# Adaptive-norm attention with mixture and zone feed-forward on one core: group 0's q and k laid at 32 rows a head, maxima from 24-row matmuls, the other layouts filled by DMA

## The chip, the core and the metric

The kernel runs on one core of one Trainium2 chip. The metric is the device time of one execution in microseconds (us). The kernel before takes 181.37 us, the median of 3 runs (181.26 to 181.59).

## The reference, cut to what matters

```python
def _L0_attn_ref(x, w_qkv, w_out):          # x: (2, 512, 128), 16 heads of 8
    q, k, v = jnp.split(x @ w_qkv.T, 3, axis=-1)
    q, k = _apply_rope(q, cos, sin), _apply_rope(k, cos, sin)
    scores = jnp.einsum('bhsd,bhtd->bhst', q, k) / scale
    scores = jnp.where(causal, scores, -jnp.inf)
    attn = jax.nn.softmax(scores, axis=-1)
    ...
    return out @ w_out.T

x = x + _L0_attn_ref(_L0_cond_ref(x, cond, weight), w_qkv, w_out)
x = x + _L0_ffn_ref(_L0_cond2_ref(x, cond, ...), ...)   # experts, then the zones chosen by a router
```

The change lies in the first microseconds of the attention, in the scores of batch 0's first four heads.

## The kernel before, in words

**Groups.** 2 batches times 16 heads are worked on in 8 groups of 4 heads (`HG = 4`, `GROUPS = 8`). Each q and k is split into a high part and a low part, both in the reduced-precision float32 format fp32r, and three part products make a score. So a head takes 8 x 3 = 24 rows (`PARTS * HD`), and a group 96 rows (`TOP`). Sequence length is 512, cut in blocks of 128.

**Two passes over the scores.** For each group TensorE first computes the scores with queries on the output partitions ("maxima units", `scores_for_max`, L1407, or L1402 for a unit of four heads), and VectorE masks and reduces each to the row maxima (`reduce_max`, L772). Then the maxima go through `max_pad` and a small matmul (`lay_max_under_q`, L1420) as 8 further rows under q. Last TensorE computes the scores again with keys on the output partitions and the maximum already subtracted (`scores_for_exp`, L1443, L1447, L1452), ScalarE takes the exponential (L1105), GpSimd masks the diagonal blocks (L672), and `weigh_v` (L1467) multiplies with v. The maxima units of group n + 1 lie between those of the exponential of group n, in an order written out by hand. Three PSUM banks in a ring hold the maxima units, so a unit waits until the unit three places before it is reduced. Of group 0's 12 maxima units all but u = 0 and u = 7 have one dummy matmul ahead (`keep_warm`, L1286).

**Layouts of q and k.** A group needs four of them. `stacked[0:96, n, :]` is k, the moving operand of the maxima units. `q_pad[n % 2]` is q once for each head, with the 72 rows of the other heads at zero, so that a 96-row matmul against all of k gives one head's scores. `q_mov[n % 3]` is q unmasked, and `k_pad[n % 3]` is k once for each head with zeros elsewhere; the exponential's matmuls use these two. For groups 1 to 7 all four are loaded by DMA from a copy in DRAM that `spill` writes from `qk_hi` and `qk_lo`. Group 0 does not go through DRAM (`BY_PE = 1`): `stack_half` (L1380, L1381) makes its 96 rows by matmul with a 0/1 pattern, in two halves of 256 columns, and ScalarE copies them out of PSUM: `place_q0(j, h)` (L1056) eight times into `q_pad[0]` with a per-row 0/1 scale, `copy_k0(h)` (L1061) into `stacked`, `copy_q0(h)` (L1065) into `q_mov[0]`. Only `k_pad[0]` is filled by DMA, from `stacked`: `pad_k(0, pairs)` (L446), two heads each time.

**SyncE's queue.** SyncE issues nearly all DMAs, strictly in the order of its program, and a wait holds up everything behind it. After group 1's spill and its loads comes: `load_k(1)`, `pad_k(0, (1,))`, `spill(sp, 2, NG, 0, spilled)` (q of groups 2 and 3 to DRAM, L390 and L393), `load_q(1)` (L461), `load_k(2)` (L455), the wait for q's spill, `pad_q(2)` (four DMAs, L433), `pad_k(1)`, `load_q(2)`, and so on. k's spill of groups 2 and 3 is issued from ScalarE's queue. `scores_for_max(2, 0)` is the first matmul that needs `pad_q(2)`. In TensorE's order it comes after group 1's twelfth maxima unit and before `scores_for_exp(0, 4)`.

Of the kernel before, what the change touches and what calls it, by code (L numbers as in the profile page):

```python
# [14 lines left out]
P = 128  # L15
# [121 lines left out]
def f32_of(ap):  # L137

    return ap.bitcast(F32)
# [7 lines left out]
def program(nc, io, scratch, out):  # L147
# [9 lines left out]
    with ctx:  # L157
# [55 lines left out]
        w_qk = raw[:, 2 * S:2 * S + 4 * D].rearrange("p (i t d) -> p i t d", i=2, t=2)  # L213
        w_v = raw[:, 2 * S + 4 * D:2 * S + 5 * D]
        w_cond = raw[:, 2 * S + 5 * D:2 * S + 6 * D]
        at = 2 * S + 6 * D
# [66 lines left out]
        def sum_of(i):  # L283
# [7 lines left out]
            pads_early ys_ready sq_ready dsum_ready dinv_ready mod_ready exp_set dvar_ready cond_ready  # L291
            qk_ready v_ready v_copied rope_ready roped_ready hi_ready lo_ready sel_zero sel_ready causal_zero q1_zero k2_zero pads_zero ones_out q_last_ready q0_placed pj_copied v_ones
            const_ready rep_ready rep_copied mx_full mx_reduced mhi_ready m_ready qm_full qm_copied st_full
# [8 lines left out]
         pads_early, ys_ready, sq_ready, dsum_ready, dinv_ready, mod_ready, exp_set, dvar_ready, cond_ready,  # L302
         qk_ready, v_ready, v_copied, rope_ready, roped_ready, hi_ready, lo_ready, sel_zero, sel_ready, causal_zero, q1_zero, k2_zero, pads_zero, ones_out, q_last_ready, q0_placed, pj_copied,
         v_ones, const_ready, rep_ready, rep_copied, mx_full, mx_reduced, mhi_ready, m_ready, qm_full, qm_copied,
# [10 lines left out]
        spilled = [sem(f"spilled_{x}") for x in "qk"]  # L315
        ld_stack = {n: [sem(f"ld_stack{x}{n}") for x in "qk"] for n in range(BY_PE, GROUPS)}
        stored = [sem(f"stored{s}") for s in range(2)]
# [65 lines left out]
        def spill(queue, first, last, i, done):  # L383
# [9 lines left out]
            queue.dma_start(parts[:, lo, :], f32_of(qk_lo[q, i, :])).then_inc(done[i], 16)  # L393

        def head_rows(j):

            return slice(j * PARTS * HD, (j + 1) * PARTS * HD)
# [15 lines left out]
        def _(sp):  # L413
# [21 lines left out]
            def pad_k(n, pairs=(0, 1)):  # L435

                s = n % BUFS
                if n >= BUFS:
                    sp.wait_ge(st_full, (n - 2) * STU)
                for h2 in pairs:  # L440
                    if n < BY_PE:
                        sp.wait_ge(rep_copied, 3)
                    for j in (2 * h2, 2 * h2 + 1):
                        q = head_rows(j)
                        src = f32_of(stacked[q, n, 0:3 * P]) if n < BY_PE else laid(n, 1)[q, 0:3 * P]
                        sp.dma_start(f32_of(k_pad[s][q, j, 0:3 * P]), src).then_inc(k_padded[s][h2], 16)  # L446

            def set_ones(s):

                sp.dma_start(f32_of(k_pad[s][TOP:ROWS, :, :]), ones_dram.rearrange("(r j) t -> r j t", j=HG)  # L450
                             ).then_inc(ones_rows[s], 16)

            def load_k(n):
# [65 lines left out]
            load_k(1)  # L519
            pad_k(0, (1,))  # L520
            spill(sp, 2, NG, 0, spilled)
            load_q(1)
            sp.wait_ge(spilled[1], 16 * SPILLS)
            load_k(2)
            sp.wait_ge(spilled[0], 16 * SPILLS)
            pad_q(2)
            sp.wait_ge(pads_zero, 2)
# [63 lines left out]
        def _(pool):  # L591
# [57 lines left out]
            def spread_last_queries(n):  # L649

                pool.wait_ge(qm_copied, n + 1)
                if n == 0:
                    pool.wait_ge(ld_head, 16)
                    pool.wait_ge(rep_copied, 4)
                else:
                    pool.wait_ge(st_full, STU * n)
                    pool.wait_ge(ld_stack[n][0], 16)
                G.tensor_tensor(q_last[0:ROWS], f32_of(q_mov[n % BUFS][0:ROWS, 3 * P:S]).unsqueeze(1).broadcast_to([ROWS, HG, P]),
                                head_mask[0:ROWS].unsqueeze(2).broadcast_to([ROWS, HG, P]),
                                ALU.mult).then_inc(q_last_ready, 1)  # L660
# [362 lines left out]
        def _(act):  # L1023
# [27 lines left out]

            def place_q0(j, h):
                act.wait_ge(rep_ready, 2 * h + 1)
                if (j, h) == (0, 0):
                    act.wait_ge(ld_const, 32)
                A.activation(q_pad[0][0:TOP, j, half(h)], first_stack(0, h)[0:TOP, :], ACT.Identity,  # L1056
                             scale=consts[0:TOP, C_HEAD + j:C_HEAD + j + 1]).then_inc(q0_placed, 1)

            def copy_k0(h):
                act.wait_ge(rep_ready, 2 * h + 2)  # L1060
                A.copy(stacked[0:TOP, 0, half(h)], first_stack(1, h)[0:TOP, :]).then_inc(rep_copied, 1)  # L1061

            def copy_q0(h):
                act.wait_ge(rep_ready, 2 * h + 1)
                A.copy(q_mov[0][0:TOP, half(h)], first_stack(0, h)[0:TOP, :]).then_inc(rep_copied, 1)  # L1065

# [139 lines left out]
            modulated(1, xc[:, 1, :], psum[:, 2, :])  # L1206
            place_q0(0, 0)
            copy_k0(0)
            take_hi_half(0, 1)
            place_q0(1, 0)  # L1210
            take_hi_half(1, 1)
            place_q0(2, 0)
            place_q0(3, 0)
            copy_q0(0)
            copy_k0(1)
            for j in range(HG):
                place_q0(j, 1)
            A.activation(minus_ident_b[:], consts[:, C_ID:C_MASK], ACT.Identity, scale=-1.0)
            A.copy(ident_r[:], consts[:, C_ID:C_MASK]).then_inc(const_ready, 1)
            copy_projection(0)  # L1220
            copy_q0(1)
            copy_v(0)
            spill(act, 2, NG, 1, spilled)
            copy_projection(1)
# [54 lines left out]
        def _(pe):  # L1279
# [25 lines left out]
            def wait_slot(*item):  # L1305

                k = ST_ORDER.index(item)
                if k < 2:
                    pe.wait_ge(q0_placed, 2 * HG)
                    pe.wait_ge(rep_copied, 4)  # L1310
                    return
                kind, n, *u = ST_ORDER[k - 2]
                if kind == "exp":
                    pe.wait_ge(exp_done, STU * n + u[0] + 1)
                else:
                    pe.wait_ge(pj_copied, n + 1)

            def wait_ring(*item):

                k = RING_ORDER.index(item)  # L1320
                if k < len(RING_BANKS):
                    if k == 1:
                        pe.wait_ge(xc_ready[1], 1)
                    elif k == 2:
                        pe.wait_ge(rep_copied, 1)
                    return
                kind, n, *u = RING_ORDER[k - len(RING_BANKS)]
                if kind == "max":
                    pe.wait_ge(mx_reduced, units_to(n, u[0] + 1))
                else:  # L1330
                    pe.wait_ge(qm_copied, n + 1)
# [23 lines left out]
            def project_v(b):  # L1355
                if b == 0:
                    pe.wait_ge(xc_ready[0], 1)
                    pe.wait_ge(q0_placed, HG)
                    pe.wait_ge(rep_copied, 2)
                else:  # L1360
                    pe.wait_ge(v_copied, KB)
# [21 lines left out]
            def scores_for_max(n, u):  # L1383
                s = n % 2
                pieces = MX_UNITS[n][u]
                if n == 0:
                    if u < 2 * HG:
                        pe.wait_ge(q0_placed, u + 1)
                    if u in (0, HG):
                        pe.wait_ge(rep_copied, 3 if u else 1)  # L1390
                elif u == 0:
                    pe.wait_ge(q_padded[s], 16 * HG * ((n + 1) // 2))
                    pe.wait_ge(ld_stack[n][1], 16)
# [4 lines left out]
                if len(pieces) == HG:  # L1398
                    pe.wait_ge(ld_stack[n][0], 16)
                    for padded in k_padded[n % BUFS]:  # L1400
                        pe.wait_ge(padded, 32 * (n // BUFS + 1))
                    last = T.matmul(bank.rearrange("p (j k) -> p j k", j=HG), q_mov[n % BUFS][0:TOP, 0:P],  # L1402
                                    k_pad[n % BUFS][0:TOP, :, 0:P], start=True, stop=True)
                else:
                    for j, qb, o in pieces:
# [18 lines left out]
            def scores_for_exp(n, u):  # L1424
                s = n % BUFS
                c, h2 = divmod(u, 2)
                if u == 0:
                    pe.wait_ge(qm_copied, n + 1)
                    if n == 0:
                        pe.wait_ge(rep_copied, 4)  # L1430
                    else:
                        pe.wait_ge(ld_stack[n][0], 16)
                    if n < BUFS:
                        pe.wait_ge(ones_rows[s], 16)
# [14 lines left out]
                else:  # L1449
                    pe.wait_ge(q1_zero, 2)  # L1450
                    pe.wait_ge(q_last_ready, n + 1)
                    last = T.matmul(ST[:, at_, :].rearrange("p (j q) -> p j q", j=HG), stacked[0:ROWS, n, 3 * P:S],  # L1452
# [246 lines left out]
def host_constants():  # L1699

    pattern = np.zeros((4, 32, P), np.float32)
    for j in range(HG):
        for d in range(HD):
            src = j * HD + d
            for t, parts in enumerate(((0, 1), (2,), (0, 2), (1,))):
                for r in parts:
                    pattern[t, src, (j * HD + d) * PARTS + r] = 1.0
    consts = np.zeros((P, C_END), np.float32)
# [71 lines left out]
```

## Time and profile before

| | |
|---|---|
| median of 3 runs | 181.37 us |
| profiled execution, its own time | 180.98 us |
| span of its trace | 179.1 us |
| TensorE busy | 168.9 us, 94% |
| VectorE busy | 138.9 us, 78% |
| ScalarE busy | 134.3 us, 75% |
| GpSimd busy | 93.8 us, 52% |
| chain that ended last, TensorE's share | 70% |

A profile line names the line of the kernel, the engine, the operation and the tiles it writes and reads. "SPq" is SyncE's queue: the time there is what it takes to issue a DMA, not to carry it out. Matmul ends are modelled, so neighbouring matmuls seem to overlap. "Landing" is the time from the issue of a DMA to its semaphore.

### The profile page before, as it was taken

Reading aid. Unit: us, or ns where it says so; the run is one execution under the profiler, and the core shown is the slowest. Engines: PE = TensorE matmul, PEld = TensorE weight load, DVE = VectorE, ACT = ScalarE, POOL = GpSimd, SP = SyncE. Lnnn points to the kernel's source line nnn. Section 1 sums busy time; section 2 is a strip of 40 time slices with the busy share of each in tenths; the row PEclk is TensorE's granted clock in tenths of the full one; section 3 lists DMA queues with packets and bytes.
Section 4 is the critical chain, followed back from the end, with each engine's and each line's share of the span. In section 5 each row is a group of like instructions: output and inputs, shape, how many; then the busy total and the mean of one; then the engine's idle time right before and its main releaser. Section 6 shows DMA issues by size and latency. Waiting matters only on the chain.

```text
span 179.1 us, 3278 instructions
## 1 busy us (share of the span) xinstructions
PE 168.9 (94%) x943; PEld 116.8 (65%) x944; DVE 138.9 (78%) x444; ACT 134.3 (75%) x224; POOL 93.8 (52%) x117
## 2 busy tenths in 40 slices
PE   6899999899999999988999999996999989999992
PEld 2656575565666666653758767864687867788881
DVE  5588989989898899980586999699799658637551
ACT  3569177688768888889734787953879999999970
POOL 5508088985463969688532522021769931676000
PEclk9999999999999999999999999999999999999999
DMA  4824775676686567520110899960760000001001
GB/s 144 294 46 107 191 203 159 218 234 213 166 267 208 143 194 194 164 94 5 62 51 17 231 345 344 347 178 4 241 230 0 0 4 0 0 2 59 0 4 59
DMA packets 15349, 24.28 MB, mean 136 GB/s; under 512 B 2844, under 2 KB 4828, under 8 KB 15308
## 3 DMA queue, kind: packets, MB, share of 16 engines
q1 hardware_dynamic: 14532, 23.29, 42.2%
q10 hardware_dynamic: 800, 0.79, 1.7%
q8 instruction: 8, 0.13, 0.3%
q14 instruction: 9, 0.07, 0.1%
HBM read 18.71 MB, written 5.27 MB: 134 GB/s over the span
## 4 chain that ended last, share of the span: by engine, by line
PE 70%; DVE 11%; ACT 7%; issue 6%; POOL 4%; DVEq 0%; ACTq 0%; POOLq 0%
PE psum L1407 11%; PE psum L1540 10%; PE psum L1541 9%; PE psum L1542 9%; PE psum L1467 8%; PE psum L1443 7%; PE psum L1286 3%; PE psum L1338 2%; PE psum L1352 2%; ACT t_probs L1105 2%; DVE psum L772 2%; DVE t_raw L924 1%; PE psum L1402 1%; ACT t_q_pad L1155 1%; PE psum L1447 1%
## 5 line engine op out<-in xcount | busy, mean ns | idle before, releaser
L772 DVE CUSTOM_DVE_ANT_0 psum<-psum,t_causal 128x128 f32<-128x128 f32 (+3 forms) x128 | 58.6, 525 | 5.8 <-PE psum L1407 3.0
L1105 ACT ACTIVATE t_probs<-psum 128x1024 f32<-128x1024 f32 (+2 forms) x48 | 40.9, 883 | 8.2 <-PE psum L1443 5.2
L1407 PE MATMUL psum<-t_stacked,t_q_pad 96*128 96x256 f32 (+2 forms) x104 | 33.3, 391 | 0.5 <-DVE t_row_max L772 0.2
L1407 PEld LDWEIGHTS psum<-t_stacked,t_q_pad 96*128 96x128 f32 x104 | 18.4, 189 | 12.4 <-DVE t_row_max L772 10.2
L672 POOL TENSOR_SCALAR_AFFINE_SELECT t_probs<-t_probs 128x512 f32<-128x512 f32 x32 | 20.5, 651 | 9.0 <-ACT t_probs L1105 9.0
L944 DVE SCALAR_TENSOR_TENSOR t_q_pad<-psum,t_zw_all,t_q_pad 128x512 fp32r<-128x512 f32 x24 | 17.8, 748 | 9.3 <-ACT t_q_pad L1153 9.2
L1139 ACT ACTIVATE psum<-psum 128x512 f32<-128x512 f32 x40 | 23.4, 586 | 0.9 <-PE psum L1542 0.3
L703 POOL TENSOR_TENSOR t_q_pad<-t_raw,t_q_pad 128x512 fp32r<-128x512 f32 x8 | 10.8, 1357 | 21.0 <-ACT t_q_pad L1155 21.0
L1467 PE MATMUL psum<-t_probs,t_v_all 128*32 128x512 f32 (+3 forms) x256 | 20.6, 439 | 0.0
L772 DVE DVE_READ_ACCUMULATOR2_ANT t_row_max<- 128x1 f32 x128 | 18.0, 141 | 0.0
L1153 ACT ACTIVATE t_q_pad<-psum,t_zw_all 128x512 fp32r<-128x512 f32 x24 | 16.5, 688 | 1.2 <-PE psum L1542 0.6
L1443 PE MATMUL psum<-t_q_two,t_k_pad 104*128 104x512 f32 (+1 forms) x48 | 13.5, 380 | 0.4 <-ACT t_q_two L1109 0.4
L1540 PE MATMUL psum<-t_stacked,t_up_hi 128*128 128x512 f32 x32 | 13.8, 430 | 0.0
L1541 PE MATMUL psum<-t_stacked,t_up_lo 128*128 128x512 f32 x32 | 12.6, 394 | 0.0
L1542 PE MATMUL psum<-t_stacked,t_up_hi 128*128 128x512 f32 x32 | 12.6, 393 | 0.0
L947 DVE TENSOR_TENSOR t_q_pad<-psum,t_q_pad 128x512 fp32r<-128x512 f32 x16 | 10.9, 680 | 1.7 <-ACT t_q_pad L1155 1.3
L931 DVE TENSOR_TENSOR psum<-psum,t_stacked 128x512 f32<-128x512 f32 x16 | 11.0, 690 | 1.4 <-DVE t_top L852 0.7
L1467 PEld LDWEIGHTS psum<-t_probs,t_v_all 128*32 128x32 f32 x256 | 6.5, 109 | 7.8 <-issue 2.9
L1155 ACT CAST t_q_pad<-psum 128x512 fp32r<-128x512 f32 x16 | 9.4, 588 | 1.2 <-DVE psum L931 1.0
L1540 PE MATMUL psum<-t_q_pad,t_dn_hi 128*128 128x512 f32 x24 | 9.8, 408 | 0.4 <-POOL t_q_pad L703 0.2
L1443 PEld LDWEIGHTS psum<-t_q_two,t_k_pad 104*128 104x128 f32 x48 | 8.4, 189 | 2.5 <-issue 0.9
L1541 PE MATMUL psum<-t_q_pad,t_dn_lo 128*128 128x512 f32 x24 | 9.5, 396 | 0.0
(233 smaller groups left out, 369.6 us busy)
## 6 DMA issues: line engine op xcount, KB each, us to landing
t_stacked<-scratch SPq DMA_DIRECT2D x16, 256.0 KB, 5.7
t_probs<-in_L_ffn_Wa SPq DMA_DIRECT2D x2, 1024.0 KB, 11.5
scratch<-t_o_sb SPq DMA_DIRECT2D x7, 256.0 KB, 2.1
t_raw<-in_experts SPq DMA_DIRECT2D x7, 256.0 KB, 3.6
t_stacked<-scratch SPq DMA_DIRECT2D x9, 192.0 KB, 3.7
t_q_pad<-scratch SPq DMA_DIRECT2D x28, 48.0 KB
scratch<-t_dn_hi SPq DMA_DIRECT2D x2, 512.0 KB, 3.4
t_q_two<-scratch SPq DMA_DIRECT2D x5, 192.0 KB, 2.6
```

Source lines behind the costliest of these rows:

```text
L672: last = G.affine_select(out=tri, in_=tri, compare_op=ALU.is_ge, fill=0.0, base=0, pattern=[[0, HG], [1, P]], channel_multiplier=-1)
L772: last = V.tensor_tensor_reduce(scores, scores, causal[:, S - width:S], 1.0, 3 * BIG, ALU.add, ALU.max, row_max[s][:, qb, j:j + 1])
L944: V.scalar_tensor_tensor(h_lo[i % SLOTS], hidden_of(i), weight_of(i), f32_of(h_hi[i % SLOTS]), ALU.mult, ALU.subtract).then_inc(lo_done, 1)
L1105: A.activation(o, scores, ACT.Exp, scale=float(1.0 / np.sqrt(np.float32(HD)))).then_inc(exp_done, 1)
L1139: A.activation(o, pair_of(i)[:, 0, :], func, scale=scale).then_inc(act_done, 1)
L1153: A.activation(h_hi[i % SLOTS], hidden_of(i), ACT.Identity, scale=weight_of(i)).then_inc(hi_done, 1)
L1407: last = T.matmul(bank[:, o:o + width], q_pad[s][0:TOP, j, qb * P:(qb + 1) * P], stacked[0:TOP, n, 0:width], start=True, stop=True)
L1443: last = T.matmul(ST[:, at_ + i, 0:S - c * P], k, q[:, c * P:S], start=True, stop=True)
L1467: last = T.matmul(PV[32 * j:32 * j + 32, lo:hi], v_all[:, v0:v0 + 32], probs[n % 2][:, c, j, o:o + hi - lo], start=(kb == 0 and lo == 0), ...
L1540: T.matmul(o, hi, x_hi, start=start, stop=False)
L1541: T.matmul(o, lo, x_hi, start=False, stop=False)
L1542: return T.matmul(o, hi, x_lo, start=False, stop=stop)
```

## The change

Group 0's stack gets 32 rows a head instead of 24: the 0/1 pattern puts head j's 24 rows at rows 32j to 32j + 23 and leaves 8 rows at zero. ScalarE copies both halves of q and of k, all 128 rows, into two free tiles, `q_rows` and `k_rows`. The maxima units of group 0 are matmuls of 24 rows at offset 32j, q of head j against k of head j, so no masked copies of q are needed: the eight `place_q0` go, and with them the semaphore `q0_placed`. The other two layouts at 24 rows a head are now filled by DMA from the two tiles: `k_pad[0]` by `pad_k(0, ...)` as before with another source, and `q_mov[0]` and the last block of k in `stacked` by eight new DMAs, `unpack_first`, in SyncE's queue ahead of `spill(sp, 2, NG, 0, spilled)`. Since nothing writes `q_pad[0]` any more before group 2's loads, ScalarE zeroes it once by a copy.

```diff
+        q_rows, k_rows = stacked[:, 14, :], stacked[:, 15, :]
...
                     if n < BY_PE:
-                        sp.wait_ge(rep_copied, 3)
+                        sp.wait_ge(rep_copied, 4)
                     for j in (2 * h2, 2 * h2 + 1):
                         q = head_rows(j)
-                        src = f32_of(stacked[q, n, 0:3 * P]) if n < BY_PE else laid(n, 1)[q, 0:3 * P]
+                        src = f32_of(k_rows[tile_rows(j), 0:3 * P]) if n < BY_PE else laid(n, 1)[q, 0:3 * P]
...
+            def unpack_first():
+
+                sp.wait_ge(rep_copied, 4)
+                for j in range(HG):
+                    sp.dma_start(f32_of(q_mov[0][head_rows(j), :]), f32_of(q_rows[tile_rows(j), :])
+                                 ).then_inc(ld_stack[0][0], 16)
+                for j in range(HG):
+                    sp.dma_start(f32_of(stacked[head_rows(j), 0, 3 * P:S]), f32_of(k_rows[tile_rows(j), 3 * P:S])
+                                 ).then_inc(ld_stack[0][1], 16)
...
             load_k(1)
             pad_k(0, (1,))
+            unpack_first()
             spill(sp, 2, NG, 0, spilled)
...
             sp.wait_ge(spilled[0], 16 * SPILLS)
+            sp.wait_ge(q0_zero, 1)
             pad_q(2)
...
-            def place_q0(j, h):
-                act.wait_ge(rep_ready, 2 * h + 1)
-                ...
             def copy_k0(h):
                 act.wait_ge(rep_ready, 2 * h + 2)
-                A.copy(stacked[0:TOP, 0, half(h)], first_stack(1, h)[0:TOP, :]).then_inc(rep_copied, 1)
+                A.copy(k_rows[:, half(h)], first_stack(1, h)).then_inc(rep_copied, 1)
...
-            place_q0(0, 0)
+            copy_q0(0)
             copy_k0(0)
             take_hi_half(0, 1)
-            place_q0(1, 0)
             take_hi_half(1, 1)
-            place_q0(2, 0)
-            place_q0(3, 0)
-            copy_q0(0)
+            copy_q0(1)
             copy_k0(1)
-            for j in range(HG):
-                place_q0(j, 1)
+            act.wait_ge(ld_const, 32)
...
-            copy_q0(1)
             copy_v(0)
+            A.copy(q_pad[0][0:TOP], f32_of(k_pad[2][0:TOP])).then_inc(q0_zero, 1)
             spill(act, 2, NG, 1, spilled)
...
+                elif n == 0:
+                    for j, qb, o in pieces:
+                        width, h = max(2 * P, P * (qb + 1)), tile_rows(j)
+                        last = T.matmul(bank[:, o:o + width], q_rows[h, qb * P:(qb + 1) * P],
+                                        k_rows[h, 0:width], start=True, stop=True)
...
                 if u == 0:
                     pe.wait_ge(qm_copied, n + 1)
-                    if n == 0:
-                        pe.wait_ge(rep_copied, 4)
-                    else:
-                        pe.wait_ge(ld_stack[n][0], 16)
+                    pe.wait_ge(ld_stack[n][0], 16 if n else 16 * HG)
...
                     pe.wait_ge(q1_zero, 2)
+                    if n == 0:
+                        pe.wait_ge(ld_stack[0][1], 16 * HG)
```

`spread_last_queries(0)` on GpSimd waits for `ld_stack[0][0]` too, instead of the fourth copy.

## Rows read from the trace of the kernel before

**Rows 1.** The page: head and busy time of each engine.
```profile
span 179.1 us, 3278 instructions
PE 168.9 (94%) x943; PEld 116.8 (65%) x944; DVE 138.9 (78%) x444; ACT 134.3 (75%) x224; POOL 93.8 (52%) x117
```

**Rows 2.** Stretches: length, then each engine's busy us, clock, DMA share, GB/s.
```profile
14.00:22.50 8.50, 8.34 (x42) 5.26 (x42) 7.85 (x34) 4.58 (x15) 4.18 (x5) 1.00 0.62 150
22.50:25.00 2.50, 2.50 (x23) 2.40 (x22) 1.92 (x12) 1.59 (x2) 2.34 (x2) 1.00 1.00 242
25.00:30.00 5.00, 4.61 (x20) 3.01 (x19) 5.00 (x21) 4.13 (x8) 4.22 (x5) 1.00 0.50 133
30.00:34.00 4.00, 3.46 (x23) 1.80 (x22) 3.50 (x15) 2.70 (x4) 3.68 (x7) 1.00 0.67 207
34.00:45.00 11.00, 10.97 (x86) 6.87 (x89) 10.22 (x43) 8.69 (x11) 8.47 (x13) 1.00 0.67 230
...
174.00:179.10 5.10, 1.91 (x9) 1.25 (x7) 1.43 (x2) 0.00 (x0) 0.00 (x0) 0.94 0.14 51
```

**Rows 3.** Timeline of VectorE (start, us, instruction, idle time before it).
```profile
14.24 0.30 DVE L772 CUSTOM_DVE_ANT_0 psum<-psum,t_causal 128x128 f32<-128x128 f32 x1 [0.36 <-PE psum L1407]
...
18.86 0.57 DVE L772 CUSTOM_DVE_ANT_0 psum<-psum,t_causal 128x384 f32<-128x384 f32 x1 [0.26 <-PE psum L1407]
...
22.80 0.30 DVE L772 CUSTOM_DVE_ANT_0 psum<-psum,t_causal 128x128 f32<-128x128 f32 x1 [0.29 <-PE psum L1407]
```

**Rows 4.** Timeline of TensorE.
```profile
13.28 0.80 PE L1407 MATMUL psum<-t_stacked,t_q_pad 96*128 96x256 f32 x2
...
24.57 0.62 PE L1443 MATMUL psum<-t_q_two,t_k_pad 104*128 104x512 f32 x2
...
29.33 0.48 PE L1407 MATMUL psum<-t_stacked,t_q_pad 96*128 96x256 f32 x2 [0.24 <-DVE t_row_max L772]
...
32.87 0.47 PE L1452 MATMUL psum<-t_stacked 104*128 104x512 f32 x1 [0.51 <-POOL t_stacked L658]
```

**Rows 5.** Timeline of ScalarE.
```profile
4.00 1.90 ACT L1030 CAST t_stacked<-t_q_pad 96x2048 fp32r<-96x2048 f32 x1
...
14.59 0.37 ACT L1061 CAST t_stacked<-psum 96x256 fp32r<-96x256 f32 x1 [0.17 <-PE psum L1381]
...
22.57 1.01 ACT L1085 COPY t_probs<-psum 128x1024 f32<-128x1024 f32 x1 [3.11 <-PE psum L1352]
```

**Rows 6.** Groups of instructions between 9 and 24 us.
```profile
L1056 ACT ACTIVATE t_q_pad<-psum,t_probs 96x256 fp32r<-96x256 f32 x8 | 3.3, 468 | 0.0
```

**Rows 7.** Timeline of SyncE's queue: start, us to issue, DMAs.
```profile
15.04 1.65 SPq L446 DMA_DIRECT2D t_k_pad<-t_stacked  x2
16.80 1.70 SPq L433 DMA_DIRECT2D t_q_pad<-scratch  x4
...
18.93 1.90 SPq L446 DMA_DIRECT2D t_k_pad<-t_stacked  x2
20.88 0.73 SPq L390 DMA_DIRECT2D scratch<-t_dn_hi  x1
21.65 0.60 SPq L393 DMA_DIRECT2D scratch<-t_dn_lo  x1
...
25.02 1.58 SPq L433 DMA_DIRECT2D t_q_pad<-scratch  x4
```

**Rows 8.** Line 446: issue ns min/median/max, first and last start.
```profile
L446 SPq DMA_DIRECT2D t_k_pad<-scratch x20: 289/364/557, 26.6 to 69.6; - x20
...
L446 SPq DMA_DIRECT2D t_k_pad<-t_stacked x4: 735/814/1102, 15.0 to 19.7; - x4
```

**Rows 9.** Line 393 (spills of low parts): issue to landing.
```profile
DMA to landing us min/median/max: 1.9/2.8/3.4
```

**Rows 10.** Line 461 (loads of q from DRAM): issue to landing.
```profile
DMA to landing us min/median/max: 2.4/2.6/4.5
```

**Rows 11.** Waits of SyncE's queue: us in total, times, longest.
```profile
SPq L433 <- DMA scratch<-t_dn_lo: 1.2, 1, 1.2
```

More of the change, by code:

```diff
@@ L291, in program @@
             pads_early ys_ready sq_ready dsum_ready dinv_ready mod_ready exp_set dvar_ready cond_ready
-            qk_ready v_ready v_copied rope_ready roped_ready hi_ready lo_ready sel_zero sel_ready causal_zero q1_zero k2_zero pads_zero ones_out q_last_ready q0_placed pj_copied v_ones
+            qk_ready v_ready v_copied rope_ready roped_ready hi_ready lo_ready sel_zero sel_ready causal_zero q0_zero q1_zero k2_zero pads_zero ones_out q_last_ready pj_copied v_ones
             const_ready rep_ready rep_copied mx_full mx_reduced mhi_ready m_ready qm_full qm_copied st_full
@@ L302, in program @@
          pads_early, ys_ready, sq_ready, dsum_ready, dinv_ready, mod_ready, exp_set, dvar_ready, cond_ready,
-         qk_ready, v_ready, v_copied, rope_ready, roped_ready, hi_ready, lo_ready, sel_zero, sel_ready, causal_zero, q1_zero, k2_zero, pads_zero, ones_out, q_last_ready, q0_placed, pj_copied,
+         qk_ready, v_ready, v_copied, rope_ready, roped_ready, hi_ready, lo_ready, sel_zero, sel_ready, causal_zero, q0_zero, q1_zero, k2_zero, pads_zero, ones_out, q_last_ready, pj_copied,
          v_ones, const_ready, rep_ready, rep_copied, mx_full, mx_reduced, mhi_ready, m_ready, qm_full, qm_copied,
@@ L315, in program @@
         spilled = [sem(f"spilled_{x}") for x in "qk"]
-        ld_stack = {n: [sem(f"ld_stack{x}{n}") for x in "qk"] for n in range(BY_PE, GROUPS)}
+        ld_stack = {n: [sem(f"ld_stack{x}{n}") for x in "qk"] for n in range(GROUPS)}
         stored = [sem(f"stored{s}") for s in range(2)]
@@ L393, in spill, with tile_rows @@
             queue.dma_start(parts[:, lo, :], f32_of(qk_lo[q, i, :])).then_inc(done[i], 16)
+        def tile_rows(j):
+            return slice(32 * j, 32 * j + PARTS * HD)
         def head_rows(j):
@@ L653, in spread_last_queries @@
                     pool.wait_ge(ld_head, 16)
-                    pool.wait_ge(rep_copied, 4)
+                    pool.wait_ge(ld_stack[0][0], 16 * HG)
                 else:
@@ L1050, in take_hi @@
                 A.copy(qk_hi[:, i, :], roped[:, i, :]).then_inc(hi_ready, 1)
-            def place_q0(j, h):
-                act.wait_ge(rep_ready, 2 * h + 1)
[L1054 to L1057, printed above, removed]
             def copy_k0(h):
                 act.wait_ge(rep_ready, 2 * h + 2)
-                A.copy(stacked[0:TOP, 0, half(h)], first_stack(1, h)[0:TOP, :]).then_inc(rep_copied, 1)
+                A.copy(k_rows[:, half(h)], first_stack(1, h)).then_inc(rep_copied, 1)
             def copy_q0(h):
                 act.wait_ge(rep_ready, 2 * h + 1)
-                A.copy(q_mov[0][0:TOP, half(h)], first_stack(0, h)[0:TOP, :]).then_inc(rep_copied, 1)
+                A.copy(q_rows[:, half(h)], first_stack(0, h)).then_inc(rep_copied, 1)
             def modulated(b, o, bank):
@@ L1308, in wait_slot @@
                 if k < 2:
-                    pe.wait_ge(q0_placed, 2 * HG)
                     pe.wait_ge(rep_copied, 4)
@@ L1324, in wait_ring @@
                     elif k == 2:
-                        pe.wait_ge(rep_copied, 1)
+                        pe.wait_ge(rep_copied, 2)
                     return
@@ L1357, in project_v @@
                     pe.wait_ge(xc_ready[0], 1)
-                    pe.wait_ge(q0_placed, HG)
-                    pe.wait_ge(rep_copied, 2)
+                    pe.wait_ge(rep_copied, 1)
                 else:
@@ L1386, in scores_for_max @@
                 if n == 0:
-                    if u < 2 * HG:
-                        pe.wait_ge(q0_placed, u + 1)
                     if u in (0, HG):
-                        pe.wait_ge(rep_copied, 3 if u else 1)
+                        pe.wait_ge(rep_copied, 4 if u else 2)
                 elif u == 0:
@@ L1706, in host_constants @@
                 for r in parts:
-                    pattern[t, src, (j * HD + d) * PARTS + r] = 1.0
+                    pattern[t, src, 32 * j + d * PARTS + r] = 1.0
     consts = np.zeros((P, C_END), np.float32)
```

## The prediction

> **What bounds the kernel now.** I read the page's head first: TensorE is busy 168.9 of 179.1 us [rows 1], so what matters is where TensorE waits, and where it would wait anew. The stretches then show which engine has slack around the change [rows 2]. From 14 to 22.5 us TensorE is busy 8.34 of 8.50, and VectorE 7.85; part of TensorE's time there is dummy matmuls, so VectorE's row maxima set the pace: it starts at 14.24 and waits only 0.26 at 18.86 and 0.29 at 22.80 [rows 3]. ScalarE, whose work the change cuts, is busy 4.58 of 8.50 [rows 2] and later sits idle for 3.11 us before 22.57 [rows 5]. From 34 to 45 us TensorE is busy 10.97 of 11.00 [rows 2], so time lost before that is not won back there. Last I read SyncE's queue [rows 7, 8, 11], because the change puts eight DMAs into it, and what is behind them feeds TensorE in its fixed order [rows 4].
>
> **ScalarE's eight masked copies go.** They are 3.3 us of work (8 x about 0.41 net) [rows 6]. The first unit needs two copies in both versions, and it starts at 13.28, behind batch 1's projection on TensorE, not behind ScalarE [rows 4]. The later units wait for their bank, that is for VectorE, which has no gap but the two named [rows 3]. Both gaps come after project_v(0) and project(1) in TensorE's order, which the change leaves. So the gain is nothing; bounds 0 and 0.26 + 0.29 = 0.55 us. I take 0. The two or three copies left grow from 96 to 128 rows at the same 256 columns, about 0.37 us each [rows 5]. The new fill of q_pad[0] is the same shape as the fill at 4.00, 1.90 us [rows 5]; it lies behind copy_v(0), in the 3.11 us idle before 22.57, so it costs nothing with 1.2 us to spare. Without that cover it would cost 1.9. ScalarE's own spill is issued behind it; if that came 1.9 us later it would still land before SyncE reaches the load that needs it.
>
> **The 24-row matmuls.** As many columns stream as before, so I price them like the 96-row ones. What no row here shows is a change between 128-row dummies and 24-row matmuls. Bounds: nothing, and one drain of some 0.2 us (what the modelled end of the two matmuls at 13.28, 0.80 us, adds beyond their streaming is of this size [rows 4]) at each of about 10 units, 2 us on TensorE. Most of it would lie in VectorE's shadow, and up to 1.6 us behind the wait for q_mov[0] below. I take 0. The Trainium skill (TensorEngine Tiling (Array Packing), Key Properties) says that changing the tiling mode drains the TensorE; by it the sum would get the 0 to 2 us of this paragraph on TensorE, no more. No run so far shows it.
>
> **The eight DMAs in SyncE's queue.** This is the term that decides. An issue of a DMA from DRAM on L446 takes 0.36 us. The four with SBUF on both sides, the form of all eight new ones, took 0.74 to 1.10, median 0.81 [rows 8]. In the queue the four, with the gaps behind them, take 16.80 - 15.04 = 1.76 and 20.88 - 18.93 = 1.95, together 3.71, so 0.93 each, while the four from DRAM right between them took 1.70, so 0.42 each [rows 7]. I take 0.93: it is the same form, at the same place. Eight are 7.4 us. The other end is 0.40 each, 3.2 us.
>
> Step by step. pad_k(0) now waits for the fourth copy, which comes about 0.1 us after the old third one (14.59 + 0.37 [rows 5]), so the queue starts 0.1 late at 15.04. unpack_first starts at about 21.0 instead of q's spill at 20.88 [rows 7]. Its four DMAs for q_mov[0] start by 21.0 + 3 x 0.93 = 23.8 and with a landing of 2.4, the least of a load [rows 10], they are there at 26.2. scores_for_exp(0, 0), which stood at 24.57 [rows 4], waits 1.6 us: the first stall. Behind it on TensorE is everything, also the maxima units that feed VectorE, which runs dry at about 25.7 and loses some 1.3 us. The four of k's last block land near 30, before line 1452 at 32.87 needs them.
>
> Behind the eight: q's spill of groups 2 and 3. Its low part is issued at 20.88 + 0.1 + 7.4 + 0.46 = 28.8 instead of 21.65 [rows 7]. Before it took 25.02 - 21.65 = 3.4 to land, and the queue waited 1.2 for it [rows 7, 11], when the DMA engines were full (1.00 from 22.5 to 25 [rows 2]). Now they are less so, since ScalarE's spill is over by then: 2.8, the median (1.9 to 3.4) [rows 9]. So pad_q(2) starts at 31.6 or 31.7, 6.6 later than 25.02. Its last DMA started at 26.2 before, landing at 28.6 by a landing of 2.4; the unit at 29.33 needed it [rows 4], so 0.7 was to spare (0 to 1.2 by landings of 3.1 to 1.9). TensorE gets to maxima unit (2, 0) 6.6 - 0.7 = 5.9 us late: the second stall, in which the first is contained. TensorE would arrive at about 29.3 + 1.3 = 30.6 and stand until 35.2.
>
> What is won back: TensorE's wait of 0.51 for GpSimd before line 1452 [rows 4] goes, since GpSimd's backlog (3.68 busy of 4.00 [rows 2]) is worked off in the stall. Less 0.5. The later loads have more to spare: pad_k(1) would land near 37 and is needed at 34.0 + 5; pad_q(3), issued at 31.2 before, would be there at 41 and be needed near 43.5.
>
> **Sum:** 0 (ScalarE) + 0 (matmuls) + 5.9 - 0.5 = 5.4 us. Against the profiled execution (180.98, of which 179.1 is span) that is a span of 184.5 and a time of 186.4; against the median of 181.37, which stands 0.4 above it, 186.8.
>
> **Rivals.**
>
> (a) The clock falls too. In the last 5.10 us of the trace, with TensorE busy 1.91 and then idle, the granted clock averages 0.94 [rows 2]: it went from its level of 2.4 GHz to that of 1.2 for the last 0.6 us, so not 3 us after the last matmul. The stall forecast at (2, 0) is 4.6 us. After it TensorE has matmuls without a pause, 10.97 of 11.00 [rows 2], and each microsecond at the lower level costs a half. If it lasts between 1 and 5 us that is 0.5 to 2.5; I take 1.5, which gives 188.3. Against it: it needs a long pause, and matmuls come soon after. The Trainium skill (TensorE: Matmul & The Clock Gate, Why this matters for your kernels) says the same: an idle gap between bursts sends the clock back to the half level. In the trace the end of the kernel agrees, and nowhere else is there such a gap.
>
> (b) Issues are cheap. If an issue between SBUF tiles costs 0.40 here (the four before were slow for another reason, say GpSimd's fills at the same time), eight are 3.2. Low part issued at 24.6, landed by 26.5 to 27.9, pad_q(2) there at 30.1 to 31.5 against 29.33: 0.8 to 2.2 late, less 0.5: 181.7 to 183.1, say 182.5. For it: 20 other issues on the same line at 0.36 [rows 8]. Against it: the DMAs from DRAM right between the slow ones took 0.42 [rows 7].
>
> (c) The other side: the DMAs are hidden and VectorE's gaps close. With an issue at 0.36 and a spill that lands in 1.9, pad_q(2) is there at about 29.8, no later than TensorE can use it, and q_mov[0] at 24.5. If then ScalarE's 3.3 us saved also removed the two gaps of 0.55, the time would be 180.8. It decides at an issue price under about 0.35 us. Against it: both gaps follow TensorE's projections, not ScalarE.
>
> (d) The mode change costs as much as its upper bound, and the DMAs as in (b): the 2 us run mostly under VectorE, leaving about 0.5: 183.
>
> **Chances.** Forecast 0.52, (a) 0.22, (b) 0.15, (d) 0.03, (c) 0.04, and 0.04 for a change that moves nothing because small gain and small loss meet. The range: issue 0.81 instead of 0.93 takes 1.0 off, a spill landing of 1.9 takes 0.9, more to spare takes 0.5, together 184.4; a landing of 3.4 adds 0.6 and no spare 0.7, with (a) 189.6. Down to 182.8 it takes in the upper half of (b). A measurement of this kernel can tell about 0.2%, 0.36 us, from no change: slower 0.91, same 0.05, faster 0.04.
>
> **What the profile after would show.** Right: eight issues from t_stacked of 0.7 to 1.1 us from about 21 us in SyncE's queue, the spill on L390 near 28.4 instead of 20.88, pad_q(2) near 31.6; in the waits, TensorE waiting for a DMA into t_q_two at the first L1443 (near 26.2) and for a DMA into t_q_pad at the 96-row unit that stood at 29.33 (now near 35); VectorE still starting near 14.2. Wrong: issues of 0.4; or TensorE late already at 22.5, which would point to the 24-row matmuls; or a granted clock under 1.00 between 31 and 40, which is (a).

## Result: 3.75% slower, and the profile after

The changed kernel takes 188.75 us (median of 4 executions, 187.09 to 190.15) against 181.48 (181.26 to 182.15): the ratio, without the longest of the four, is 1.0375 with a 95% interval of 1.034 to 1.0409. 186.8 was forecast, with a range of 182.8 to 189.6. The profiled execution is that longest one, 190.15 us; the four differ in how long the clock was low (mean granted clock 0.964, 0.972, 0.991, 0.972).

The page of the changed kernel, head and slices (40 equal slices of 4.7 us):

```profile
span 188.4 us, 3273 instructions
PE 178.7 (95%) x944; PEld 119.8 (64%) x944; DVE 139.9 (74%) x444; ACT 133.5 (71%) x217; POOL 93.7 (50%) x117
...
PEclk9999555999999999999999999999999999999999
```

TensorE is 9.8 us busier than in [rows 1] with the same number of matmuls but one. The clock row says most of why: three slices at the half level, which the kernel before does not have. The stretches from 14 us on are cut as in [rows 2] up to 34 us, and the columns are those of [rows 2] (length, busy us of TensorE, its weight loads, VectorE, ScalarE and GpSimd, then clock, DMA share, GB/s):

```profile
14.00:22.50 8.50, 8.50 (x32) 5.02 (x31) 4.79 (x22) 2.49 (x9) 4.12 (x5) 0.77 0.43 107
22.50:25.00 2.50, 2.50 (x6) 0.75 (x5) 1.38 (x4) 2.02 (x3) 0.00 (x0) 0.50 0.72 154
25.00:30.00 5.00, 5.00 (x8) 1.94 (x8) 2.63 (x8) 0.00 (x0) 1.05 (x1) 0.50 0.46 96
30.00:34.00 4.00, 4.00 (x24) 3.11 (x23) 1.65 (x11) 1.59 (x2) 2.70 (x3) 0.72 0.67 188
34.00:38.00 4.00, 3.86 (x16) 2.46 (x14) 4.00 (x19) 2.87 (x5) 1.57 (x2) 1.00 0.47 133
```

TensorE is busy without a gap from 14 to 34 us, and its clock is nevertheless at 2.4 GHz only until some 3.9 us before 22.5 (the clock averages 0.77 there, and each microsecond at the half level takes off a half: 0.23 x 8.5 / 0.5), then at 1.2 GHz into the stretch from 30 to 34. Together that is 3.9 + 2.5 + 5.0 + 2.2 = 13.6 us. VectorE, which had 7.85 of 8.50 in [rows 2], has 4.79: it is no longer what sets the pace. Its timeline shows some of its waits for TensorE, 2.00 and 2.95 us long, against 0.26 and 0.29 in [rows 3]:

```profile
14.70 0.30 DVE L789 CUSTOM_DVE_ANT_0 psum<-psum,t_causal 128x128 f32<-128x128 f32 x1 [0.88 <-PE psum L1409]
...
22.58 0.57 DVE L789 CUSTOM_DVE_ANT_0 psum<-psum,t_causal 128x384 f32<-128x384 f32 x1 [2.00 <-PE psum L1409]
...
31.76 0.30 DVE L789 CUSTOM_DVE_ANT_0 psum<-psum,t_causal 128x128 f32<-128x128 f32 x1 [2.95 <-PE psum L1414]
```

TensorE's timeline (L1292 is the dummy, L1409 the 24-row unit, L1357 project(1), L1447 the first matmuls of the exponential, L1414 unit (2, 0)):

```profile
15.05 0.39 PE L1292 MATMUL psum<-t_warm 128*128 128x512 bf16 x1
15.37 0.50 PE L1409 MATMUL psum<-t_stacked 24*128 24x256 f32 x2
15.80 0.39 PE L1292 MATMUL psum<-t_warm 128*128 128x512 bf16 x1
16.12 0.50 PE L1409 MATMUL psum<-t_stacked 24*128 24x256 f32 x2
...
23.74 0.61 PE L1292 MATMUL psum<-t_warm 128*128 128x512 bf16 x1
24.27 0.79 PE L1409 MATMUL psum<-t_stacked 24*128 24x512 f32 x1
...
27.51 3.78 PE L1357 MATMUL psum<-t_raw 128*128 128x512 f32 x4
...
33.76 0.63 PE L1447 MATMUL psum<-t_q_two,t_k_pad 104*128 104x512 f32 x2
...
38.60 0.47 PE L1414 MATMUL psum<-t_stacked,t_q_pad 96*128 96x256 f32 x2 [0.25 <-DVE t_row_max L789]
```

In the kernel before, project(1) stands here:

```profile
20.65 1.88 PE L1352 MATMUL psum<-t_raw 128*128 128x512 f32 x4
```

The dummy goes from 0.39 to 0.61 us and project(1) from 1.88 to 3.78 us: that is how a halved clock looks in the rows. Unit (2, 0) is at 38.60 instead of 29.33 [rows 4], 9.3 us late, and the span is 9.3 us longer. Everything is lost before this point, and it waits there for VectorE, not for a DMA.

SyncE's queue, beside [rows 7] (L462 and L465 are the eight new DMAs, L391 the spill, L438 pad_q(2)):

```profile
21.20 3.10 SPq L462 DMA_DIRECT2D t_q_two<-t_stacked  x4
24.34 3.21 SPq L465 DMA_DIRECT2D t_stacked<-t_stacked  x4
27.59 0.70 SPq L391 DMA_DIRECT2D scratch<-t_dn_hi  x1
...
31.62 1.51 SPq L438 DMA_DIRECT2D t_q_pad<-scratch  x4
```

The queue did what was forecast: eight issues in 6.4 us (7.4 forecast), pad_q(2) at 31.62 (31.6 or 31.7 forecast). Only, TensorE came later than the data: in this trace it waits for no DMA between 11 and 60 us. If the queue has a price of its own, it lies under the other delay, and the trace of the change can't show it; the parts have to be run alone.

### The profile page after: what moved, and what is told of

Read it like the earlier page. It is cut to its first block, busy times and chain, and to the rows that moved or that the text cites. A ratio compares the mean times of both kernels' runs of the same rounds, so it can differ in the third digit from the quotient of the medians.

```text
span 188.4 us, 3273 instructions
## 1 busy us (share of the span) xinstructions
PE 178.7 (95%) x944; PEld 119.8 (64%) x944; DVE 139.9 (74%) x444; ACT 133.5 (71%) x217; POOL 93.7 (50%) x117
## 4 chain that ended last, share of the span: by engine, by line
PE 71%; DVE 11%; ACT 7%; issue 5%; POOL 4%; DVEq 0%; ACTq 0%; POOLq 0%
PE psum L1546 9%; PE psum L1414 9%; PE psum L1547 8%; PE psum L1548 8%; PE psum L1473 8%; PE psum L1447 6%; PE psum L1292 4%; PE psum L1409 3%; PE psum L1357 3%; PE psum L1343 2%; ACT t_probs L1115 2%; PE psum L1369 2%; DVE psum L789 2%; DVE t_raw L941 1%; PE psum L1404 1%
## 5 line engine op out<-in xcount | busy, mean ns | idle before, releaser
L1414 PE MATMUL psum<-t_stacked,t_q_pad 96*128 96x256 f32 (+2 forms) x88 | 27.8, 386 | 0.5 <-DVE t_row_max L789 0.2
L1414 PEld LDWEIGHTS psum<-t_stacked,t_q_pad 96*128 96x128 f32 x88 | 15.6, 195 | 12.5 <-DVE t_row_max L789 10.2
L1447 PE MATMUL psum<-t_q_two,t_k_pad 104*128 104x512 f32 (+1 forms) x48 | 13.6, 381 | 0.4 <-ACT t_q_two L1119 0.4
L1447 PEld LDWEIGHTS psum<-t_q_two,t_k_pad 104*128 104x128 f32 x48 | 8.5, 189 | 2.4 <-issue 0.9
L1292 PE MATMUL psum<-t_warm 128*128 128x512 bf16 x18 | 8.6, 557 | 1.4 <-POOL t_warm L610 1.4
```

The source lines that it names most:

```text
L1414: last = T.matmul(bank[:, o:o + width], q_pad[s][0:TOP, j, qb * P:(qb + 1) * P], stacked[0:TOP, n, 0:width], start=True, stop=True)
L1447: last = T.matmul(ST[:, at_ + i, 0:S - c * P], k, q[:, c * P:S], start=True, stop=True)
```

## The experiments

**1. The 24-row matmuls alone.** The kernel before; in `scores_for_max`, for group 0:

```diff
+                        at_ = 32 * (0, 1, 2, 1)[j]
+                        h = slice(at_, at_ + PARTS * HD) if n == 0 else slice(0, TOP)
-                        ... q_pad[s][0:TOP, j, qb * P:(qb + 1) * P], stacked[0:TOP, n, 0:width] ...
+                        ... q_pad[s][h, j, qb * P:(qb + 1) * P], stacked[h, n, 0:width] ...
```

> The kernel before with one edit: group 0's maxima matmuls take 24 rows of the old tiles (offsets 0, 32, 64, 32 for the four heads) instead of 96, so they compute only a part of those scores, with the same columns, order, waits, masked copies and DMAs as before. Theory M (the 24-row matmuls cost the time: about 0.3 us a unit for going between 128-row dummies and 24-row units, and the granted clock falls to the half level while TensorE is busy): 187 to 190 us, clock below 1.00 from near 19 us, no other change needed. Theory Q (SyncE's queue, as predicted, costs the time): 181.2 to 182.0, clock 1.00.

Measured: 187.38 us median, but no execution lies there; they are of two kinds: 183.81 and 184.50 with clocks of 0.999 and 0.997, 190.27 and 190.35 with 0.964. The profiled one is the first kind, so its trace shows the matmuls' cost without the clock's. One stretch and its timeline, then two dummies of the kernel before with a unit of 512 columns between them:

```profile
14.00:22.50 8.50, 8.50 (x36) 4.51 (x35) 6.55 (x27) 4.53 (x15) 4.13 (x5) 1.00 0.50 116
```
```profile
15.05 0.50 PE L1409 MATMUL psum<-t_stacked,t_q_pad 24*128 24x256 f32 x2
15.48 0.39 PE L1286 MATMUL psum<-t_warm 128*128 128x512 bf16 x1
15.80 0.49 PE L1409 MATMUL psum<-t_stacked,t_q_pad 24*128 24x256 f32 x2
16.22 0.39 PE L1286 MATMUL psum<-t_warm 128*128 128x512 bf16 x1
...
32.27 0.49 PE L1409 MATMUL psum<-t_stacked,t_q_pad 96*128 96x256 f32 x2 [0.24 <-DVE t_row_max L772]
```
```profile
18.67 0.39 PE L1286 MATMUL psum<-t_warm 128*128 128x512 bf16 x1
19.14 0.39 PE L1286 MATMUL psum<-t_warm 128*128 128x512 bf16 x1
```

A unit with its dummy takes 16.22 - 15.48 = 0.74 us, against 19.14 - 18.67 = 0.47 in the kernel before. TensorE, busy 8.50 of 8.50 us, sets the pace and not VectorE (6.55), and unit (2, 0) is 2.9 us later than in [rows 4]. With the clock down it is another 5.8 to 6.5 us: the two kinds are 183.81 and 184.50, and 190.3. No DMA was changed, and where the clock falls to 0.964 this edit alone reaches the time of the whole change at the same clock, 190.15. So theory M's two costs are there, the second in half of the executions.

**2. The eight DMAs alone.** The kernel before with `copy_q0` and `copy_k0` into two other tiles and `unpack_first` in the queue, with 24 rows a head at both ends:

```diff
             pad_k(0, (1,))
+            unpack_first()
             spill(sp, 2, NG, 0, spilled)
```

> The kernel before with the eight unpacking DMAs and their waits added at the same place in SyncE's queue (24 rows a head at both ends), masked copies and 96-row matmuls kept. Theory Q: eight issues of 0.78 us with gap, 6.3 us, put pad_q(2) near 31.3; less 0.7 to spare and 0.5 won back: 181.4 + 5.1 = 186.5 (184.5 to 188), clock fall possible in the stall. Theory M with the DMAs hidden for good: 181.2 to 182.0. If both costs are real and lie over each other, this and the run with 24-row matmuls alone add up to more than the change's +7.3 us.

Measured: 188.11 us (187.15 to 188.66), ratio 1.036 (1.0322 to 1.0397), clock 0.970 to 0.982. TensorE's timeline and stretches:

```profile
26.82 0.70 PE L1452 MATMUL psum<-t_q_two,t_k_pad 104*128 104x512 f32 x2 [1.73 <-issue]
...
35.35 0.79 PE L1419 MATMUL psum<-t_stacked,t_q_pad 96*128 96x256 f32 x2 [2.95 <-DMA t_q_pad<-scratch]
```
```profile
25.00:30.00 5.00, 3.07 (x12) 2.27 (x12) 3.44 (x17) 1.94 (x2) 2.20 (x3) 0.90 0.14 32
30.00:34.00 4.00, 2.40 (x7) 1.59 (x5) 2.73 (x9) 2.19 (x6) 2.89 (x4) 0.50 0.81 207
34.00:38.00 4.00, 2.65 (x14) 1.56 (x14) 0.87 (x4) 0.96 (x2) 3.04 (x4) 0.50 0.56 155
```
```profile
28.00:29.00 1.00, 0.85 (x4) 0.37 (x2) 0.99 (x5) 1.00 (x2) 0.00 (x0) 0.99 0.05 12
29.00:30.00 1.00, 0.95 (x3) 0.85 (x4) 1.00 (x5) 0.49 (x1) 0.44 (x1) 0.50 0.30 68
```

Both stalls of the prediction are there, ending at 26.82 (26.2 forecast; the trace names no releaser, but `ld_stack[0][0]` is the one wait that the edit puts before that matmul) and at 35.35 (35.2 forecast). The eight issues took 7.2 us, where this experiment's expectation had 6.3, and unit (2, 0) is 6.0 us later than in [rows 4]. The clock falls too, but not in the stall where rival (a) had it: it falls at 29.0, 2.2 us after the first stall ended and with TensorE at work again, and stays at the half level through the second. The time is that of rival (a), 188.3; against this experiment's own expectation it is 0.1 above the range of 184.5 to 188. The queue's cost is as real as the matmuls'. Alone the DMAs cost 6.8 us, their clock fall included, and the matmuls 2.8 where the clock stayed and 8.9 to 9.0 where it fell (median 6.0); the change with both costs 7.3, not the sum.

**3. The change with nothing new ahead of the spill.** q's four DMAs go to ScalarE's queue, k's four behind pad_q(2):

```diff
             pad_k(0, (1,))
-            unpack_first()
...
             pad_q(2)
+            unpack_first()                      # k's half
...
+            for j in range(HG):                 # in ScalarE's program, ahead of copy_v(0)
+                act.dma_start(f32_of(q_mov[0][head_rows(j), :]), f32_of(q_rows[tile_rows(j), :])
+                              ).then_inc(ld_stack[0][0], 16)
             copy_v(0)
```

> The changed kernel with the q half of the unpacking issued from ScalarE's queue ahead of copy_v(0) and the k half from SyncE's queue behind pad_q(2), so that nothing new stands ahead of the spill. Theory M: the time stays that of the changed kernel, 187 to 190.5, because TensorE reaches unit (2, 0) late by itself. Theory Q: it falls to 181.5 to 183.5.

Measured: 190.27 us median (185.97 to 190.68), three executions with a clock of 0.964 and one with 0.991. Unit (2, 0) in its trace:

```profile
38.45 0.48 PE L1414 MATMUL psum<-t_stacked,t_q_pad 96*128 96x256 f32 x2 [0.24 <-DVE t_row_max L785]
```

Taking the DMAs out of the way gives nothing back, as theory M says: with a clock of 0.964 it is at 189.99 to 190.68, the change at 190.15. One hint that they count where the clock falls late: the executions with a clock of 0.991 are at 187.09 in the change and 185.97 here; that is one of each.

**4. What holds the clock: no dummies, 96 rows.** `keep_warm(1, bank)` ahead of group 0's units is taken out of the kernel before.

> The kernel before without the ten dummy matmuls ahead of group 0's maxima units. Theory M1 (what keeps the granted clock up is the rows and columns that matmuls drive; the 96-row units give enough of it alone): clock stays 1.00, time 181.0 to 181.6. Theory M2 (the dummies are what holds the clock, and 24-row units only dilute them): the clock falls between 17 and 25 us and the time is 183 to 189.

Measured: 180.89 us (10 executions, 180.40 to 181.69), ratio 0.9976 (0.9962 to 0.999), so 0.24% faster; clock 0.998 or more in all ten. Its first stretch, and unit (2, 0):

```profile
14.00:22.50 8.50, 7.42 (x34) 4.74 (x33) 7.90 (x35) 5.00 (x16) 4.25 (x5) 1.00 0.59 155
```
```profile
30.07 0.50 PE L1405 MATMUL psum<-t_stacked,t_q_pad 96*128 96x256 f32 x2 [0.95 <-DMA t_q_pad<-scratch]
```

TensorE is busy 7.42 of 8.50 us and keeps 2.4 GHz; in the changed kernel it was busy 8.50 of 8.50 and lost it. So pauses are not why the changed kernel loses the clock, and the ten dummies were not what held it. The clock is that of M1, and the time lies 0.1 us below its range.

**5. 24-row dummies at the unit's own offset.** On top of experiment 1:

```diff
-                    keep_warm(1, bank)
+                    g = 32 * (0, 1, 2, 1)[pieces[0][0]]
+                    T.matmul(bank, warm[g:g + 24, 0:P], warm[g:g + 24, :], start=True, stop=True)
```

> As the kernel with 24-row matmuls alone, but the ten dummies too take 24 rows, at the unit's own offset, so TensorE does not go between 128-row and 24-row matmuls within a unit; streamed columns are the same. Theory S (the lost 0.3 us a unit is the change of the array's tiling): a unit of one dummy and one matmul takes about 0.45 us at the full clock again and VectorE sets the pace: 181.2 to 182.2 in executions whose clock stays. Theory R (what brings the clock down is how many rows the matmuls drive): the clock falls in all or most executions and the median is 184 to 188. If pauses from the changes of tiling brought the clock down, it stays at 1.00 here and the time is 181.2 to 182.2 throughout.

Measured: 186.19 us (184.87 to 186.33), ratio 1.0267, clock 0.972 to 0.981 in all five executions. Timeline, then the stretches:

```profile
15.75 0.39 PE L1398 MATMUL psum<-t_warm 24*128 24x512 bf16 x1
15.79 0.58 PE L1410 MATMUL psum<-t_stacked,t_q_pad 24*128 24x256 f32 x2
...
16.83 0.37 PE L1398 MATMUL psum<-t_warm 24*128 24x512 bf16 x1 [0.46 <-DVE t_row_max L772]
```
```profile
14.00:22.50 8.50, 7.87 (x40) 4.46 (x39) 6.95 (x30) 4.99 (x16) 4.24 (x5) 0.85 0.56 134
22.50:25.00 2.50, 2.50 (x4) 1.11 (x4) 1.22 (x6) 0.00 (x0) 1.06 (x1) 0.50 0.96 200
```

Unit and dummy now start 0.04 us apart (15.75 and 15.79) instead of 0.32 (15.48 and 15.80), and TensorE waits 0.46 for VectorE again at 16.83. The 0.28 us a unit go with the changes between 128-row and 24-row matmuls, as theory S says; its time of 181.2 to 182.2 could not be seen, since the clock stayed in no execution. It falls with those changes gone, so they are not what brings it down; that is theory R's side. In the stretch above it is at 0.85 with TensorE busy 7.87 of 8.50.

**6. 24 rows without dummies, and 7. the same in the changed kernel with split queues.** The dummies are taken out of experiments 1 and 3.

> 24-row matmuls alone, without the ten dummies, so few changes of tiling are left. Theory S: units are not paced by TensorE and 181 to 182 where the clock stays. Theory R: the array is driven even less than with the dummies, so the clock falls in nearly all executions and near 17 to 22 us; TensorE at the half level has less to do than with dummies, 183 to 187.

> The changed kernel with both costs cut: unpacking DMAs behind the spill (as in the run with split queues) and no dummies. Theory: without changes of tiling and with nothing ahead of the spill it is at 181.0 to 182.0 where the clock stays, and 183 to 187 where it falls, the latter more often; in no case faster than the kernel before by over 0.5 us, because VectorE's row maxima from 14.2 us on are the same.

Measured: 185.07 us (184.42 to 186.04), ratio 1.0223 (1.0184 to 1.0262), clock 0.972 to 0.981; and 185.93 us (184.71 to 187.14), ratio 1.0253 (1.0204 to 1.0302), clock 0.971 to 0.981. The clock fell in all eight executions. The first stretch of experiment 6, then three of experiment 7:

```profile
14.00:22.50 8.50, 7.25 (x30) 4.29 (x30) 7.21 (x32) 4.92 (x16) 4.24 (x5) 0.83 0.60 141
```
```profile
14.00:22.50 8.50, 6.99 (x29) 4.34 (x27) 6.39 (x29) 4.50 (x10) 3.71 (x5) 0.72 0.55 144
22.50:25.00 2.50, 2.50 (x4) 1.12 (x4) 1.48 (x6) 0.00 (x0) 0.80 (x1) 0.50 0.94 191
25.00:30.00 5.00, 5.00 (x27) 4.09 (x26) 2.33 (x15) 1.87 (x3) 2.96 (x3) 0.70 0.52 151
```

Experiments 4 and 6 differ in nothing but the rows of group 0's maxima matmuls. TensorE is busy 7.42 and 7.25 of 8.50 us, nearly the same, and the clock stayed in ten of ten executions with 96 rows and in none of four with 24. That the rows decide here is shown by this pair. With tiling changes, dummies and queue all taken care of, the change is still 2.5% slower. In experiment 7's trace the clock is at the half level for 4.8 + 2.5 + 3.0 = 10.3 us, which is up to 5.1 us of time; the 4.5 us that it is above the kernel before fit into that.

**8. Two 128-row dummies a unit.** Experiment 1 with `keep_warm(2, bank)`.

> 24-row matmuls alone, with two 128-row dummies ahead of each of the ten units instead of one. Theory R (rows driven hold the clock): the clock stays at 0.998 or more in all or nearly all executions, and the time is that of the execution with one dummy whose clock stayed, 183.8, plus ten dummies of 0.23 us: 185.5 to 186.7, with little spread. If the clock falls for another reason (the pauses at a change of tiling), it falls as often as with one dummy, half the executions, and those are at 190 to 193.

Measured: 187.09 us (186.46 to 187.31), ratio 1.0303, clock 0.997 or more in all four executions. A unit takes 0.97 us from dummy to dummy:

```profile
17.03 0.60 PE L1286 MATMUL psum<-t_warm 128*128 128x512 bf16 x2
17.57 0.50 PE L1409 MATMUL psum<-t_stacked,t_q_pad 24*128 24x256 f32 x2
18.00 0.61 PE L1286 MATMUL psum<-t_warm 128*128 128x512 bf16 x2
```

As many tiling changes as with one dummy, twice the 128-row matmuls, and no fall. None of four against two of four is thin by itself, but experiment 5, where the changes are gone and the clock falls, points the same way: it is not the pauses at the changes. The time is 0.4 us above the range expected; in this trace TensorE waits 0.94 us for a load into `q_pad` at 53.13, which it does not in experiment 1.

**9. and 10. Is there more to have in the queue?** On top of experiment 4, q's spill ahead of `pad_k(0, (1,))`; and, instead, the two DMAs of `pad_k(0, (1,))` on ScalarE's queue ahead of `copy_projection(0)`. The edit of experiment 9:

```diff
-            pad_k(0, (1,))
             spill(sp, 2, NG, 0, spilled)
+            pad_k(0, (1,))                      # experiment 9
```

> The kernel before without the ten dummies, and with q's spill issued ahead of pad_k(0, (1,)) instead of behind it. If what stands ahead of the spill is what delays pad_q(2), this pulls it 1.6 us forward, takes the wait of 0.95 us before maxima unit (2, 0) away, and gives 180.2 to 180.8, 0.2 to 0.6 below the run without dummies alone. If it only moves the wait to the second half of k_pad[0], 180.9 to 181.6.

> The kernel before without the ten dummies and with the second half of k_pad[0] issued from ScalarE's queue instead of SyncE's, so SyncE reaches q's spill about 1.9 us earlier without moving anything behind it. If pad_q(2) is what TensorE still waits for there, 180.2 to 180.8; if ScalarE's issues hold up copy_projection(0) or copy_v(0), or k_pad[0] comes late again, 181 to 184 with clock falls.

Measured: 183.72 us (12 executions, 181.40 to 186.06) and 181.20 us (12 executions, 180.53 to 181.85; ratio 0.9992, 0.9975 to 1.0009). Moving the spill only moved the wait, to the second half of `k_pad[0]`, and the clock fell in six of the twelve executions (0.972 to 0.981); with the clock at 0.998 or more they took 181.40 to 183.65, so most lie above the 180.9 to 181.6 expected for that case. TensorE in experiment 9's trace:

```profile
26.99 0.73 PE L1441 MATMUL psum<-t_q_two,t_k_pad 104*128 104x512 f32 x2 [1.67 <-DMA t_k_pad<-t_stacked]
```

In experiment 10 pad_q(2) is in time, TensorE waits for VectorE there (0.24) as in [rows 4], and nothing is gained. Both expectations of a gain were misses. Experiment 4 has the lowest median, though its interval and that of experiment 10 overlap.

## Why the prediction was right, and where its steps failed

The sign and the size were right (186.8 forecast, 188.75 measured), but partly by luck. The forecast comes wholly from the queue. In the changed kernel neither forecast stall happens: TensorE comes late to unit (2, 0) by itself, and the time is that of a term put at 0 and of a clock that falls without a stall. That these come near the queue's price (6.8 us alone, against 7.3 for the change) could not be read from the prediction.

**ScalarE's copies.** No gain was forecast and none is seen. No run takes only the copies out; but experiment 7, without them, is not faster than experiment 6, with them. VectorE's start, forecast at about 14.2, was 14.70; 0.27 of that is no effect of the change, for ScalarE's `modulated(1, ...)`, which comes ahead of these copies, already starts at 11.39 against 11.12 before.

**The 24-row matmuls.** This is the step that failed: "I take 0", with up to 2 us hidden under VectorE. Measured at the full clock, going between 128 and 24 rows and back costs 0.28 us a unit (0.32 - 0.04; from dummy to dummy 0.74 against 0.47), which makes TensorE slower than VectorE and moves unit (2, 0) by 2.9 us. The upper bound of 2 us for ten units was too low (2.8 by the measured price); worse was to hide it behind VectorE: TensorE, busy 8.34 of 8.50 us [rows 2], had no room for ten such prices. Rival (d) had the mode change at its bound, but also mostly under VectorE, and at a chance of 0.03. The Trainium skill (TensorEngine Tiling (Array Packing), Key Properties) says that changing the mode drains the engine. The runs agree as far as they go: the change of mode costs 0.28 us. That a drain is what takes it, they do not show.

**The clock.** Rival (a) had the clock fall in a stall, and held against it that it needs a long pause. In the changed kernel it fell with TensorE busy throughout, and cost 6.4 us of the 9.3 (9.3 less the 2.9 of experiment 1), over 13.6 us at the half level, which at a half for each would be 6.8. Nothing in the prediction allowed for that. A fall behind a wait is seen in experiment 2, 2.2 us after one of 1.73 us. But waits are not the whole of it: experiment 4 waits 0.95 us ahead of unit (2, 0) and keeps the clock, and the changed kernel, without a wait, loses it.

**SyncE's queue.** The mechanism was right: pad_q(2) at 31.62, and by itself 188.11 us, which is the forecast with rival (a) (188.3). That pad_q(2) is right to the tenth is luck, though. The issues took 0.80 with gap and not 0.93, 1.0 us less for eight; the queue reached them 0.2 later, the spill's second DMA came 0.75 behind its first where the sum had 0.46 ([rows 7] has 0.77), and the spill took 3.3 and not 2.8 to land. Rival (b), cheap issues, and with it (c), are out: the form with SBUF on both sides costs 0.7 us and more at that place and time. Nor were GpSimd's fills the reason, as (b) proposed: GpSimd is idle from 22.5 to 25 us of the changed kernel (0.00 of 2.50), and the issues still take 0.71 or more. In the change this cost lies under the other: data that arrives 6.6 us late harms nobody when TensorE is 9.3 late.

**The tell-tales.** Of the signs named for being right, those in SyncE's queue came (the spill at 27.59, 0.8 us early) and TensorE's two waits for a DMA did not. The sign of (a), a clock under 1.00 between 31 and 40, came only as the last 1.2 us of the low stretch. The prediction said that TensorE late already at 22.5 would point to the 24-row matmuls. It was: group 0's units last until 27.5 in the changed kernel, and in [rows 3] VectorE is already on group 1 at 22.80.

What stays open: why the clock falls in two of four executions of experiment 1, in all of the changed kernel and of experiment 3 with the same number of dummies, and for different lengths of time. The runs do not tell; each program has one trace.

## What to carry to other kernels

Before narrowing a matmul to save copies on another engine, look at who sets the pace and at what stands next to it on TensorE: each change between wide and narrow row tiles cost time here, and a run of narrow matmuls cost the clock although the engine was never idle. Count the DMAs that a new layout adds to an in-order queue and follow what is behind them to the first matmul that needs it. And when a forecast comes out right, look whether the forecast waits are in the trace, and run the parts alone: two costs here lay over each other, and the one that was forecast could not be seen in the whole.

## What the runs showed of the hardware that was not expected

- TensorE's granted clock fell from 2.4 to 1.2 GHz in the middle of work: 8.50 of 8.50 us busy, at 0.77 in that stretch. With 24-row matmuls and no 128-row dummies among them it fell in 13 of 13 executions (experiments 5 to 7), with one dummy a unit in 2 of 4 (experiment 1) and in all 8 of the changed kernel and experiment 3, with two in none of 4, and with 96-row matmuls and no dummies in none of 10.
- In the traces of experiments 2 and 9 a wait of TensorE of 1.7 us is followed by a fall of the clock; in experiment 2 it came 2.2 us after the wait, with TensorE at work again. In experiment 9 the clock fell in six of twelve executions.
- A change between 128-row and 24-row matmuls and back costs 0.28 us.
- Issuing a DMA between two SBUF tiles took SyncE 0.71 us (median of the four on L462 and of the four on L465; up to 0.94 there, and the eight of experiment 2 took 7.2 us where these took 6.4) against 0.36 from DRAM at the same number of rows [rows 8]; on ScalarE's queue it was 0.74 and 1.62.
